# A graph layer with a gated FFN on one core: the FFN computed behind the loop, for the selected tokens alone

## The reference

```
xn = layernorm(x)
x  = x + gnn(xn, src, dst) + mix(xn)          # called x2 in the kernel
xf = layernorm(x)                             # called x3
# gnn: top 32 of each row of xn @ W_neigh are kept, summed over the edges
#      of each destination, divided by its number of edges; plus xn @ W_self
# mix: linear attention with a sigmoid gate, projected by Wproj
weights = xf @ wr + br                        # one number a token
_, idx  = top_k(weights, 3125);  sel = idx[:3124]
h = gelu(xf[sel] @ w1 + b1)                   # 256 -> 1024
y = (h @ w2 + b2) * weights[sel]              # 1024 -> 256
out = x + xf + scatter(y at sel)
```

## Time and profile before

| | |
|---|---|
| median of 3 runs | 2461.32 us (2454.12 to 2475.36) |
| profiled execution, span | 2470.0 us |
| loop over the positions | about 437 to 2404 us |
| threshold search | 2406 to 2441 us |
| mask, combine and last stores | 2441 to 2470 us |
| TensorE busy | 1713.3 us (69%) |
| VectorE busy | 1289.5 us (52%) |
| GpSimd busy | 1068.1 us (43%) |
| ScalarE busy | 456.7 us (18%) |

### The profile page before, as it was taken

The page is one execution under the profiler, slowest core; times in us unless marked ns, Lnnn a source line. Parts: engine busy times, 40 slices in busy tenths (PEclk is TensorE's granted clock), DMA queues, the critical chain, the costliest instruction groups (busy, mean ns, idle before and its releaser), DMA issues. The chain is left out here.

```text
span 2470.0 us, 40137 instructions
## 1 busy us (share of the span) xinstructions
PE 1713.3 (69%) x8913; PEld 1213.6 (49%) x8914; DVE 1289.5 (52%) x4086; ACT 456.7 (18%) x1009; POOL 1068.1 (43%) x1156
## 2 busy tenths in 40 slices
PE   1985556766556676667677767777767778776873
PEld 0552442444335454445455545545545656555662
...
GB/s 168 68 77 55 124 61 64 71 75 79 85 75 103 153 74 65 76 167 75 66 101 138 59 75 178 57 70 184 50 67 186 49 72 165 68 72 149 90 77 188
DMA packets 173360, 239.30 MB, mean 97 GB/s; under 512 B 34148, under 2 KB 141950, under 8 KB 173214
## 3 DMA queue, kind: packets, MB, share of 16 engines
...
## 5 line engine op out<-in xcount | busy, mean ns | idle before, releaser
L717 POOL DMA_INDIRECT ring<-rows_d,stage x960 | 948.4, 988 | 1174.9 <-PE bank L1062 812.0
L1062 PE MATMUL bank<-ring,region_v 128*125 x1120 | 399.5, 463 | 115.5 <-issue 108.3
L1036 PE MATMUL bank<-region_k 128*125 x830 | 291.6, 456 | 184.1 <-issue 164.7
L1530 DVE TENSOR_SCALAR col_deg<-bank 125x1 f32<-125x1 f32 x50 | 7.9, 158 | 610.9 <-remote 321.9
L1466 DVE TENSOR_SCALAR region_k<-iota,win_start,region_k 128x500 f16 x830 | 305.1, 407 | 29.7 <-issue 26.4
L1439 DVE SCALAR_TENSOR_TENSOR region_v<-iota,tile_start,dstT 128x500 f16 x280 | 205.6, 739 | 182.7 <-issue 144.4
L1062 PEld LDWEIGHTS bank<-ring,region_v 128*125 x1120 | 171.5, 153 | 246.0 <-issue 185.7
L1022 PE MATMUL bank<-region_v 128*125 128x256 f32 x848 | 243.5, 440 | 68.6 <-issue 68.3
L1014 PE MATMUL bank<-region_v 128*128 128x125 f32 x1664 | 230.8, 295 | 73.4 <-issue 72.8
L1036 PEld LDWEIGHTS bank<-region_k 128*125 x830 | 114.6, 151 | 312.0 <-issue 299.7
L1014 PEld LDWEIGHTS bank<-region_v 128*128 128x128 f32 x1664 | 222.9, 210 | 87.9 <-issue 84.6
...
## 6 DMA issues: line engine op xcount, KB each, us to landing
...
```

The lines of the kernel that those rows point to most:

```text
L717: pool.indirect_dma_start(out=ring[:, c, :], out_offset=None, in_=rows_d, in_offset=bass.IndirectOffsetOnAxis(ap=stage[:, c:c + 1], axis=0 ...
L1036: m = pe.matmul(out, lo, key, start=False, stop=False, skip_group_check=True)
L1062: m = pe.matmul(total, onehot_s, row_s, start=False, stop=False, skip_group_check=True)
```

## The change

The FFN leaves the loop. In each position VectorE now writes a row buffer of 516 numbers a token: x3 (256), x2+x3 (256) and the weight, and raises s_res at the end of its chain. ScalarE waits for that and issues two stores: the whole buffer to kept_d in DRAM (258 KB), and x2+x3 straight to the output (125 KB). keep_x3T, the GELUs, ffn_rows, w_at and the store of yw go, as do turn_x3, ffn_up and ffn_down in TensorE's position.

Behind the search, VectorE counts ranks: for each token how many selected ones stand before it, cut into a tile (0 to 24) and a place in it (0 to 124). From one-hots of both, 50 matmuls (125x125 by 125x50) make `slots`, for each of 25x125 places the number of its token. GpSimd gathers 25 tiles of rows by these numbers (258 KB each). They are worked on in 7 teams, six of 4 tiles and one of 1: per team 8 transposes, ffn_up as 16 matmuls of 500 columns, ffn_down as 8 matmuls a tile. ffn_up of a team comes ahead of ffn_down of the one before. VectorE adds bias and weighted product to the gathered x2+x3, and GpSimd scatters each tile to the output. 50 combines, the loads of yw and the 10 block stores are gone. A few semaphores of the prologue are merged, and b2 is loaded after the loop.

The core of the diff (definitions of keep_x3T, hidden, turn_x3, ffn_up and ffn_down of before, which are removed, stand above; of the merged semaphores and the tile declarations nothing is shown):

```diff
+    SEL = -(-KEEP // T)
+    WIDE = 4
+    RW = 2 * C + 4
+    TEAMS = [range(j, min(j + WIDE, SEL)) for j in range(0, SEL, WIDE)]
...
+            pool.wait_ge(s_hotB, 1)
+            pool.tensor_tensor(tile_ids[:, :, SEL:2 * SEL], tile_hot,
+                               iota[0:T, 0:NT].rearrange("p (t a) -> p t a", a=1).to_broadcast([T, NT, SEL]), ALU.mult)\
+                .then_inc(s_idw, 1)
+            for p in range(2):
+                pool.wait_ge(s_rowout[p], 32 * (NT // 2 + 1))
+            pool.wait_ge(s_slots, 1)
+            for g, team in enumerate(TEAMS):
+                for j in team:
+                    pool.indirect_dma_start(
+                        out=row_of(j), out_offset=None, in_=kept_d,
+                        in_offset=bass.IndirectOffsetOnAxis(ap=slots[:, j:j + 1], axis=0)).then_inc(s_kept[g], 16)
+            for j in range(SEL):
+                held = min(T, KEEP - j * T)
+                pool.wait_ge(s_fin, j + 1)
+                pool.indirect_dma_start(
+                    out=out_d, out_offset=bass.IndirectOffsetOnAxis(ap=slots[0:held, j:j + 1], axis=0),
+                    in_=row_of(j)[0:held, C:2 * C], in_offset=None).then_inc(s_out, 16)
...
-                hidden(one)
-                keep_x3T(one)
+                act.wait_ge(s_m3, two)
...
                 gate_hidden(n + 2)
-                act.wait_ge(s_yw, one)
-                act.dma_start(yw_t[:, bass.ds(n, 1), :], yw[:, s % 2:s % 2 + 1, :]).then_inc(s_ywout[s % 2], 16)
+                act.wait_ge(s_res, one)
+                act.dma_start(kept_t[:, bass.ds(at.tile, 1), :], rowbuf[:, s % 2:s % 2 + 1, :]).then_inc(s_rowout[s % 2], 16)
+                act.dma_start(out_t[:, bass.ds(at.tile, 1), :], rowbuf[:, s % 2:s % 2 + 1, C:2 * C]).then_inc(s_rowout[s % 2], 16)
...
+            act.wait_ge(s_hotB, 1)
+            act.activation(tile_ids[:, :, 0:SEL], tile_hot, ACT.Identity, scale=pidx[:, 0:1]).then_inc(s_idw, 1)
+
+            def hidden(g):
+                wide = len(TEAMS[g]) * T
+                if g > 1:
+                    act.wait_ge(s_y, 2 * (g - 1))
+                for n in range(NH):
+                    act.wait_ge(s_up, g * NH + n + 1)
+                    act.activation(hid[:, g % 2, n, 0:wide], up_bank(n)[:, 0:wide], ACT.Gelu_apprx_tanh,
+                                   bias=b1[:, n:n + 1]).then_inc(s_hid, 1)
+
+            for g in range(len(TEAMS)):
+                hidden(g)
...
-                pe.wait_ge(s_yw, here)
                 pe.wait_ge(s_pfree, here)
-                ffn_down(one, y_sum)
                 ends.look_ahead(at_)
-                ffn_up(one)
                 spans.look(at_)
...
-                    turn_x3(one)
                     from_rows(summed[r][-1])
...
-            thirds = ((0, 3), (3, 6), (6, NH))
-            assert ROUNDS_D == 7 + len(thirds)
...
-                if i < 3:
-                    ffn_up(NT + 2, *thirds[i])
-                elif i < 6:
-                    pe.wait_ge(s_yw, NT + 1)
-                    ffn_down(NT + 2, y_sum, *thirds[i - 3])
-                elif i > 6:
-                    ffn_down(NT + 3, p_sum, *thirds[i - 7])
...
-            pe.matmul(bank[1][0:T, 0:NT], ones[0:T, 0:T], eqm, start=True, stop=True)
-            pe.matmul(bank[2][0:T, 0:NT], upper[:], eqm, start=True, stop=True).then_inc(s_tot, 1)
+            pe.matmul(bank[1][0:T, 0:2 * NT], ones[0:T, 0:T], masks, start=True, stop=True)
+            pe.matmul(bank[2][0:T, 0:2 * NT], upper[:], masks, start=True, stop=True).then_inc(s_tot, 1)
+
+            pe.wait_ge(s_idw, 2)
+            pe.wait_ge(s_gate, NT + 1)
+            for t in range(NT):
+                pe.wait_ge(s_hotA, t + 1)
+                m = pe.matmul(bank[3][0:T, 0:2 * SEL], rank_hot[:, t, :], tile_ids[:, t, :], start=(t == 0), stop=(t == NT - 1))
+            m.then_inc(s_ids, 1)
+
+            def turn_x3(g):
+                pe.wait_ge(s_kept[g], 16 * len(TEAMS[g]))
+                if g:
+                    pe.wait_ge(s_x3T, g)
+                for u, j in enumerate(TEAMS[g]):
+                    for k in range(KC):
+                        m = pe.transpose(bank[k][:, u * T:(u + 1) * T], row_of(j)[:, k * 128:(k + 1) * 128], ident[0:T, 0:T])
+                m.then_inc(s_tx3, 1)
+
+            def ffn_up(g, first=0, end=NH):
+                wide = len(TEAMS[g]) * T
+                pe.wait_ge(s_x3T, g + 1)
+                for n in range(first, end):
+                    if g * NH + n >= 4:
+                        pe.wait_ge(s_hid, g * NH + n - 3)
+                    for k in range(KC):
+                        m = pe.matmul(up_bank(n)[:, 0:wide], w1[:, k, n * 128:(n + 1) * 128], x3T[:, g % 2, k, 0:wide],
+                                      start=(k == 0), stop=(k == KC - 1))
+                    m.then_inc(s_up, 1)
+
+            def ffn_down(g):
+                pe.wait_ge(s_hid, (g + 1) * NH)
+                for h in range(2):
+                    if g:
+                        pe.wait_ge(s_yfree, 2 * (g - 1) + h + 1)
+                    mine = range(len(TEAMS[g]))[2 * h:2 * h + 2]
+                    if not mine:
+                        continue
+                    for u in mine:
+                        for n in range(NH):
+                            m = pe.matmul(y_pair(h)[:, u % 2, :], hid[:, g % 2, n, u * T:(u + 1) * T], w2[:, n, :],
+                                          start=(n == 0), stop=(n == NH - 1))
+                    m.then_inc(s_y, 1)
+
+            pe.wait_ge(s_slots, 1)
+            turn_x3(0)
+            ffn_up(0, 0, NH - 2)
+            turn_x3(1)
+            ffn_up(0, NH - 2, NH)
+            for g in range(1, len(TEAMS)):
+                ffn_up(g)
+                if g + 1 < len(TEAMS):
+                    turn_x3(g + 1)
+                ffn_down(g - 1)
+            ffn_down(len(TEAMS) - 1)
...
-                dve.wait_ge(s_y, one)
                 dve.wait_ge(s_p, one)
                 st.after(a)
                 dve.tensor_tensor(base_p, base_x, p_sum, ALU.add).then_inc(s_pfree, 1)
-                hold(dve, s_ywout[u], (half + 1) * 16)
-                ffn_rows(st, n, y_sum, yw[:, u, :], one)
...
-                hold(dve, s_tx3, one)
+                hold(dve, s_rowout[u], (half + 1) * 32)
                 a = st.mark(dve.tensor_scalar(x3, x2, mv[:, 0:1], col["rstd"][:, 0:1], ALU.subtract, ALU.mult))
                 st.after(a)
-                dve.sem_inc(s_x3, 1)
-
                 a = st.mark(dve.tensor_tensor_reduce(out=junk, in0=x3, in1=wr, scale=1.0, scalar=0.0, op0=ALU.mult,
                                                      op1=ALU.add, accum_out=col["w"][:]))
-                dve.tensor_tensor(res_all[:, bass.ds(tile, 1), :], x2.rearrange("p (a c) -> p a c", a=1),
-                                  x3.rearrange("p (a c) -> p a c", a=1), ALU.add).then_inc(s_res, 1)
+                b = st.mark(dve.tensor_tensor(rowbuf[:, u, C:2 * C], x2, x3, ALU.add))
...
-                a = st.mark(dve.tensor_scalar(w_at[:, bass.ds(n + 3, 1)], col["w"][:], br[:, 0:1], None, ALU.add))
+                a = st.mark(dve.tensor_scalar(rowbuf[:, u, 2 * C:2 * C + 1], col["w"][:], br[:, 0:1], None, ALU.add))
                 if s + 1 < PER:
                     hold(dve, *st.at(a))
                 else:
                     st.after(a)
+                dve.sem_inc(s_res, 1)
...
+            gtm, eqm = masks[:, 0:NT], masks[:, NT:2 * NT]
...
+            above, equal = prefix[:, 0:NT], prefix[:, NT:2 * NT]
+            b = st.mark(dve.scalar_tensor_tensor(out=rank, in0=equal, scalar=c["need"], in1=above, op0=ALU.min, op1=ALU.add))
+            d = st.mark(dve.scalar_tensor_tensor(out=hit, in0=equal, scalar=c["need"], in1=eqm, op0=ALU.is_lt, op1=ALU.mult))
             st.after(b)
-            b = st.mark(dve.tensor_tensor(selm, hit, gtm, ALU.add))
+            a = st.mark(dve.tensor_scalar(rough, rank, -float(T // 2), 1.0 / T, ALU.add, ALU.mult))
+            st.after(d)
+            d = st.mark(dve.tensor_tensor(selm, hit, gtm, ALU.add))
+            st.after(a)
...
+            dve.scalar_tensor_tensor(out=tile_hot, in0=iota[0:T, 0:SEL].rearrange("p (a j) -> p a j", a=1).to_broadcast([T, NT, SEL]),
+                                     scalar=1000.0, in1=rough.rearrange("p (t a) -> p t a", a=1).to_broadcast([T, NT, SEL]),
+                                     op0=ALU.add, op1=ALU.is_equal).then_inc(s_hotB, 1)
+            st.after(a)
             for t in range(NT):
-                dve.scalar_tensor_tensor(out=res_all[:, t, :], in0=yw_all[:, t, :], scalar=selm[:, t:t + 1],
-                                         in1=res_all[:, t, :], op0=ALU.mult, op1=ALU.add).then_inc(s_fin, 1)
+                dve.tensor_scalar(rank_hot[:, t, :], iota[0:T, 0:T], rank_in[:, t:t + 1], None, ALU.is_equal).then_inc(s_hotA, 1)
+            dve.wait_ge(s_ids, 1)
+            a = st.mark(dve.tensor_copy(rank, bank[3][0:T, 0:NT]))
+            st.after(a)
```

(29 more changed lines are left out.)

268 lines of the change are left out of this document (107 added, 161 removed).

## The result

The changed kernel takes 2576.9 us (median of 4 runs, 2567.1 to 2592.5) where the kernel before, timed beside it, takes 2466.4: a ratio of **1.049**, 95% interval 1.041 to 1.058. Slower, by 110 us. Ratios in this text are those of the record; medians are of all runs, so their quotient can differ by half a per cent (1.045 here). The forecast was 2535 us and slower, with 2411 to 2616 as its range. The sign holds and so does the price of the end; the loop gained 78 us where 125 were forecast. Timed once more on another chip of the same speed the ratio was 1.050 (1.045 to 1.055). Single executions of some kernels ran several per cent longer at a lower granted clock (2536.9 us at 0.57 for the one with fewer FFN matmuls, where the others took 2354 to 2392); the ratios leave these out.

What follows compares the result with a forecast made beforehand. VectorE waits for TensorE at each position's end, but most FFN work lies beside VectorE's layer norm. Profiled 2470+199-125 = 2544, so 2535 us; own range 2480 to 2590, 8 in 10 from 2411 to 2616.

Steps and rivals of the forecast that it cites:

- The tail: After the loop: the FFN on gathered tiles replaces the combines, +199 us, between 185 and 215.
- Sparse positions, head: Loop: first visits move up to the first one-hot; that margin (distance between them, less 0.74) gains 132 us, capped.
- Sparse positions, rest: Loop, visits: less dense work ahead of them lowers TensorE's clock, charged at 12 us.
- Dense positions: Loop, 8 positions: the late x load leaves about 0.6 us of gain each, 5 us in all, bounds -20 to +36.
- the loop gains 132+5-12 = 125 us: Whole loop: sparse positions 132, dense positions 5, less 12 for the clock; between 60 and 240.
- rival C: ScalarE's queue: the s_res wait ahead of x loads lengthens dense and short positions, 4.5 us by 8, 2571 us; chance 0.15.
- Rival A: Loop: TensorE's stream is the bound throughout; price up to 589 us, with 350 the time is 2310; chance 0.20.
- Rival B: Loop: mean clock 0.68 instead of 0.82 costs visits and window counts 131 us, half exposed, 2600 us; chance 0.15.

Runs made afterwards that it cites:

- the early loads: Changed kernel with the next position's x, xT and scale loads issued before the s_res wait and row stores, except every tenth position: 2529.8 us, 1.033 of before.
- the short FFN: Kernel before with 11 full-width FFN matmuls a position instead of 24 (output wrong): 2377.5 us, 0.967 of before.
- the kernel with 4 columns: Kernel before with the moving side of every FFN matmul in the loop cut to 4 columns: 2006.3 against 1951.1 us on the faster chip.

## Why the prediction was right, and where it wasn't

- **The tail**: +199 forecast; from the last degree step to the end the changed kernel takes 261.4 us (2318.9 to 2580.3), the kernel before 72.8 (2397.2 to 2470.0): **+189**. TensorE's part was 17 us too high: a down-projection of a tile took 3.5 us (87.3 us for 25, where 92.5 were forecast), 8 transposes 0.85 at the upper clock (0.11 each, not 0.205), and the start, stalls and copies cost less than the 6 us set aside. 16 matmuls of 500 columns took 13.4 (0.84 each, 0.89 forecast) at the upper clock; the first 12 took 13.2, since they begin at the lower one. First gathers and the end were 6 us too low.
- **Sparse positions, head**: 132 us of capped margin forecast; the heads shortened by 121 us in the first pair of traces and by 146 in the second. The margins of 41 sparse positions sum to 144 us in the trace of before and to 17 in the first one of the changed kernel: the first one-hot is what releases the first visit. This step is right.
- **Sparse positions, rest**: forecast to lose 12 us to the clock. They lost 48 and 67. With the early loads the two traces show 9 and 31 us over the mean of the two of the kernel before; with the short FFN 37 on its own pair. So, within the spread of 20 to 40 us, something between a tenth and a third of an earlier first visit is given back. How much of it is clock stays open. The granted clock of the rests was 0.78 before and 0.75 after, and visits and window counts (L1062 and L1036 of the earlier trace rows) took 43 us more of TensorE:

```profile
L1056 PE MATMUL bank<-ring,region_v 128*125 x1067 | 408.5, 485 | 156.6 <-issue 94.5 <-DVE region_v L1457 59.9
L1030 PE MATMUL bank<-region_k 128*125 x738 | 270.5, 465 | 154.4 <-issue 108.8 <-DVE region_k L1484 40.0
```

- **Dense positions**: +5 us of gain forecast, with -20 to +36 as bounds. Measured 0 and -9. The late x was seen and its landing at 14 us forecast; the eight reads of `bounds` behind it in three of the positions were not, and they had cost nothing only because VectorE waited. With x early these positions give 25 us.
- **The term that was mis-sized** is thus "the loop gains 132+5-12 = 125 us": it gained 72 and 70 us between the same degree steps (1959.8 to 1887.3, 1947.6 to 1877.7), and 6 to 8 more ahead of the first, 78 in all. The heads came out as forecast, and the sum was too large by 47, by the rests above all. The tail's ten too many hid part of it: 47-10 is 37 of the 42 us by which the median missed the forecast, and that is luck. (The other 5: the changed kernel's trace lies 3.4 us above its median, not 8.7.) Of the 47 the early loads return 47 us, which is rival C: it had a chance of 0.15 as an alternative, where its price belonged into the forecast. In the dense positions alone that price is 25 us, inside its 36; that late loads would cost sparse positions nothing was wrong by some 11 us at the short ones; for the remaining 11 or so no trace names a place.
- **A reading that was wrong**: the 610.9 us in which VectorE stands still ahead of the degree step are not all waiting for TensorE. In 27 of 41 sparse positions the closing matmul (L1146) had ended over 0.5 us before, by 215 us in all (167 in the other trace of the kernel before), and in 172 of these GpSimd was issuing gathers. The longest, from the timelines of TensorE, GpSimd and VectorE:

```profile
766.80 0.25 PE L1146 MATMUL bank<-zeros 128*125 128x2 f16 x1 [1.26 <-issue]
...
783.54 0.95 POOL L717 DMA_INDIRECT ring<-rows_d,stage  x1 [0.30 <-issue]
...
789.18 0.16 DVE L1530 TENSOR_SCALAR col_deg<-bank 125x1 f32<-125x1 f32 x1 [30.57 <-remote]
```

  On the faster chip (the kernel with ffn_up among the visits) it is 18 us. So on the slower chips a good part of the rests is neither TensorE's work nor VectorE's, and taking work from TensorE cannot shorten it.
- **Rival A** (TensorE's stream is the bound throughout) is refuted twice: 307 us of its busy time went for 72 us, and 370 us put back cost 30.
- **Rival B**: the clock fell as the Trainium skill has it ("TensorE: Matmul & The Clock Gate", section "HAM oscillation — how this bites in real kernels": idle gaps between bursts bring the lower clock back), from 0.82 to 0.72 over the loop. The trace agrees in the position above: 5.41 us idle, then the mixer at the lower clock. The price in the heads was nothing, since the mixer ends before the one-hot; the kernel with 4 columns shows 55 us where it doesn't. In the visits it is not settled.

No kernel here that computes the whole layer beats the one before. The changed one with early loads is 3% slower. What is still exposed in it is the 180 us of TensorE behind the loop.
